# Last pair of a fused graph kernel: the attention result of group 0 finished by ScalarE and GpSimd instead of VectorE, with a new order of the last side work

## The chip, the cores and the metric

One core of a Trainium2 chip runs the whole kernel. The metric is the device time of one launch in microseconds (us). The profile shows one execution, with TensorE (PE), its weight loads (PEld), VectorE (DVE), ScalarE (ACT), GpSimd (POOL) and SyncE's DMA queue (SP) on one clock.

## The reference

For each of 128 graphs of 128 nodes with 256 features (f32):

```python
h = relu(layernorm(x))
for i in range(3):                       # gated graph network
    m = h @ weight[i]; aggr = A.T @ m    # A = (adj != 0)
    h = gru_cell(aggr, h, w_ih, w_hh, b_ih, b_hh)
x = x + h
h = relu(layernorm(x))                   # graph attention
Wh = h @ W.T
e = leaky_relu((Wh @ a1)[:, :, None] + (Wh @ a2)[:, None, :], 0.2)
att = softmax(where(adj == 0, -inf, e)); att = where(adj == 0, 0, att)
x = x + att @ Wh
```

## The kernel before, in words

Four graphs make a group, two groups (0 and 1) a pair, and there are 16 pairs. A pair runs through six slots: slot s works on group s % 2 in layer s // 2. Each slot has eight steps, hn0, r0, in0, z0, hn1, r1, in1, z1: the products of one gate for one half of the features, into a PSUM bank of the gate's own. ScalarE applies tanh, VectorE combines (`gate`, `update`). The state is kept in f16 high and low parts, so each product is three f16 matmuls.

All else is side work that is put between the steps: the neighbour sums (`neighbours`: PE, then an eviction by ACT, then the low part by DVE), the turning of the state by DMA, and the attention of the pair before (offset -1): norm, dot products, scores, softmax, `gather`, `attend`. Nothing orders it but tables written out by hand, `SIDE` for most pairs and `LAST` for the last pair. An entry such as `(4, 7): [("attend", 1, 0, -1)]` says that the engine does that stage, for group 1, half 0, of the pair before, after step 7 of slot 4. Each engine runs its own table strictly in order, and semaphores join them. So an entry that is moved also moves what is queued behind it on its engine. Key (6, 0) stands behind the last gate.

The last pair's own attention has nothing behind it to hide under, and has stages of its own, with f32 products. For group a and half h (two graphs), in the order of their needs:

- `residual` (PE L1088 turns the state, DVE L1382 adds it to x), `stats_att` (DVE L451), `tail_norm` (DVE L1494 to L1505, with a power on POOL, L1579), `tail_apply` (ACT L1276, the normed and clipped features);
- `tail_turn` (PE L1148), `tail_ut` (ACT L1290, out of PSUM), `tail_wh` (PE L1157, the product with W; the weights are put together once by POOL, L1582), `tail_out` (ACT L1296, out of PSUM);
- `tail_dots` (DVE L1511, two dot products per graph), `tail_row` (PE L1134, spreads one of them along a row), `tail_mask` (DVE L1520), `tail_scores` (DVE L1532 to L1545), `tail_softmax` (ACT L1284), `tail_scale` (DVE L1550 to L1554, one over the row sums, for a whole group);
- `tail_probs` (PE L1166, turns the probabilities), `tail_pt` (ACT L1302 or DVE L1481, out of PSUM), `tail_attend` (PE L1175), `tail_finish` (DVE L1461: product times row scale plus x, one instruction per graph), `tail_store` (SP L982).

Each half has its own PSUM banks. In the table before, DVE evicts `tail_pt` for half 1 of group 1 alone, and ACT the other three; all four `tail_finish` are DVE's.

Of the kernel before, what the change touches and what calls it, by code (L numbers as in the profile page):

```python
# [39 lines left out]
D = 256  # L40
# [176 lines left out]
        (4, 2): [("attend", 0, 1, -1), ("neighbours", 1, 2, 0, 0)],  # L217
        (4, 5): [("neighbours", 1, 2, 1, 0), ("gather", 1, 0, -1)],
        (4, 6): [("residual", 0, 0, 0)],
        (4, 7): [("gather", 1, 1, -1), ("attend", 1, 0, -1)],  # L220
        (5, 0): [("residual", 0, 1, 0)],
        (5, 1): [("attend", 1, 1, -1)],
        (5, 5): [("tail_row", 0, 0, 0)],
        (5, 7): [("tail_turn", 0, 0, 0), ("residual", 1, 0, 0), ("residual", 1, 1, 0), ("tail_probs", 0, 0, 0),
                 ("tail_turn", 0, 1, 0), ("tail_wh", 0, 0, 0), ("tail_row", 0, 1, 0), ("tail_attend", 0, 0, 0),
                 ("tail_wh", 0, 1, 0), ("tail_turn", 1, 0, 0), ("tail_turn", 1, 1, 0), ("tail_row", 1, 0, 0),
                 ("tail_wh", 1, 0, 0), ("tail_row", 1, 1, 0), ("tail_probs", 0, 1, 0), ("tail_wh", 1, 1, 0)],
        (6, 0): [("tail_probs", 1, 0, 0), ("tail_attend", 0, 1, 0), ("tail_attend", 1, 0, 0),
# [56 lines left out]
        (4, 0): [("neighbours", 0, 2, 1, 0), ("attend", 0, 0, -1), ("scores", 1, -1), ("update", 1, 1, 1, 0),  # L285
                 ("split_state", 1, 2, 1, 0), ("split_probs", 1, -1)],
        (4, 3): [("neighbours", 1, 2, 0, 0), ("attend", 0, 1, -1), ("update", 0, 2, 0, 0),
                 ("neighbours", 1, 2, 1, 0)],
        (4, 4): [("gather", 1, 0, -1)],
        (4, 5): [("residual", 0, 0, 0)],  # L290
        (4, 6): [("tail_mask", 0, 0), ("update", 0, 2, 1, 0), ("gather", 1, 1, -1), ("attend", 1, 0, -1),
                 ("residual", 0, 1, 0)],
        (4, 7): [("stats_att", 0, 0), ("tail_norm", 0, 0), ("attend", 1, 1, -1)],
        (5, 3): [("tail_dots", 0, 0, 0), ("tail_dots", 0, 1, 0), ("update", 1, 2, 0, 0)],
        (5, 4): [("tail_mask", 1, 0)],
        (5, 6): [("tail_scores", 0, 0, 0), ("update", 1, 2, 1, 0), ("residual", 1, 0, 0), ("residual", 1, 1, 0),
                 ("stats_att", 1, 0)],
# [40 lines left out]
def per_chunk(p, a, c):  # L338
    return p * 4 + 2 * a + c + 1
# [1274 lines left out]
```

## Time and profile before

| | |
|---|---|
| time, median of 3 runs (lowest to highest) | 1752.26 us (1751.38 to 1753.65) |
| time of the profiled execution, its span | 1753.62 us, 1751.8 us |
| PE busy | 1737.6 us, 99% of the span |
| DVE busy | 1489.7 us, 85% |
| ACT busy | 1106.5 us, 63% |
| POOL busy | 312.3 us, 18% |
| last gate product starts, last instruction on DVE starts | 1729.06 us, 1748.31 us |

An engine's row gives what it was busy in all. A kernel that keeps PE at 99% can only differ, under this change, in its last slots and behind the last gate; so the timelines of each engine are to be read there, item by item: start, duration, what it writes and reads, and in brackets how long the engine stood idle before and what released it. Durations of neighbouring items overlap a little, so the step from one start to the next is the cost of an item on a busy engine.

### The profile page before, as it was taken

The page shows a single profiled execution, that of the slowest core. Times are in us where ns is not written, and L with a number is a line of the kernel's source. Part 1 is how long each engine was busy: PE and PEld are TensorE (multiplying, and loading weights), DVE is VectorE, ACT ScalarE, POOL GpSimd, SP SyncE. Part 2 cuts the span into 40 slices and gives each one's busy share as a digit, 9 for nine tenths or more (in the row PEclk, how much of TensorE's full clock was granted, in tenths as well). Part 3 has the DMA queues.
Part 4 walks back from the last instruction along what each step waited for, and adds up shares of the span by engine and source line. Part 5 has one row for each costly group of instructions (what it writes and reads, how often), then busy time and mean ns, then how long its engine had stood idle before and what let it go on. Part 6 is the DMA issues. An engine that isn't in the chain of part 4 may idle for free. (4 is left out here: it accounts for less than half of the span.)

```text
span 1751.8 us, 32025 instructions
## 1 busy us (share of the span) xinstructions
PE 1737.6 (99%) x10109; PEld 907.3 (52%) x10109; DVE 1489.7 (85%) x2914; ACT 1106.5 (63%) x2009; POOL 312.3 (18%) x759
## 2 busy tenths in 40 slices
PE   8999999999999999999999999999999999999998
PEld 6444555545555454554545555455554545545455
DVE  6678898888988888888888988889888888888888
ACT  6566656666566666666666666665666666666664
POOL 2022022211212112021120222112121120211200
PEclk9999999999999999999999999999999999999999
DMA  4235352344425334253343523445243342533332
GB/s 121 67 61 103 80 125 43 90 106 88 111 42 116 82 84 111 42 123 84 72 114 75 123 48 82 109 90 114 42 112 86 84 108 42 122 85 74 79 67 67
DMA packets 393648, 152.03 MB, mean 87 GB/s; under 512 B 305280, under 2 KB 389776, under 8 KB 393616
## 3 DMA queue, kind: packets, MB, share of 16 engines
q1 hardware_dynamic: 393616, 151.64, 38.9%
q8 instruction: 16, 0.26, 0.1%
q14 instruction: 16, 0.13, 0.0%
HBM read 60.83 MB, written 16.84 MB: 44 GB/s over the span
## 5 line engine op out<-in xcount | busy, mean ns | idle before, releaser
L1203 ACT ACTIVATE n_out<-n_pre,smalls 128x512 f32<-128x512 f32 x192 | 137.8, 718 | 191.3 <-DVE n_pre L1330 190.6
L552 ACT ACTIVATE nb_hi<-nb_bank 128x512 f16<-128x512 f32 x192 | 114.1, 594 | 215.0 <-PE nb_bank L538 215.0
L523 PE MATMUL hn_bank<-ht_s,wh_hi 128*128 128x512 f16 x768 | 228.4, 379 | 0.0
L523 PE MATMUL r_bank<-ht_s,wh_hi 128*128 128x512 f16 x768 | 228.4, 379 | 0.0
L523 PE MATMUL z_bank<-ht_s,wh_hi 128*128 128x512 f16 x768 | 228.4, 379 | 0.0
L1198 ACT ACTIVATE tanh_r<-r_bank,b_rz,down 128x512 f32<-128x512 f32 x192 | 148.6, 774 | 112.4 <-PE r_bank L523 112.4
L1323 DVE SCALAR_TENSOR_TENSOR n_pre<-tanh_r,hn_b 128x512 f32<-128x512 f32 x192 | 147.3, 767 | 78.5 <-ACT tanh_r L1198 76.4
L556 DVE TENSOR_TENSOR nb_lo<-nb_bank,nb_hi 128x512 f16<-128x512 f32 x192 | 131.4, 684 | 47.5 <-ACT nb_hi L552 47.5
L1574 POOL TENSOR_TENSOR ht<-ht_s 128x512 f32<-128x512 f16 x64 | 85.9, 1342 | 467.3 <-DMA ht_s<-h_s 353.0
L1193 ACT ACTIVATE hn_b<-hn_bank,b_hn,down 128x512 f32<-128x512 f32 x192 | 147.9, 770 | 19.0 <-PE hn_bank L523 18.9
L1207 ACT ACTIVATE tanh_z<-z_bank,b_rz,down 128x512 f32<-128x512 f32 x192 | 147.6, 769 | 19.2 <-PE z_bank L523 19.0
L1330 DVE SCALAR_TENSOR_TENSOR n_pre<-in_bank,down,n_pre 128x512 f32<-128x512 f32 x192 | 143.1, 745 | 17.3 <-PE in_bank L523 14.8
L1343 DVE SCALAR_TENSOR_TENSOR diff<-tanh_z,diff 128x512 f32<-128x512 f32 x192 | 143.6, 748 | 10.6 <-ACT tanh_z L1207 3.5
L523 PE MATMUL hn_bank<-ht_s,wh_lo 128*128 128x512 f16 x384 | 145.5, 379 | 0.0
L523 PE MATMUL r_bank<-ht_s,wh_lo 128*128 128x512 f16 x384 | 145.5, 379 | 0.0
L523 PE MATMUL r_bank<-nb_hi,wi_hi 128*128 128x512 f16 x384 | 145.5, 379 | 0.0
L523 PE MATMUL r_bank<-nb_lo,wi_hi 128*128 128x512 f16 x384 | 145.5, 379 | 0.0
L523 PE MATMUL r_bank<-nb_hi,wi_lo 128*128 128x512 f16 x384 | 145.5, 379 | 0.0
L523 PE MATMUL in_bank<-nb_hi,wi_hi 128*128 128x512 f16 x384 | 145.5, 379 | 0.0
L523 PE MATMUL in_bank<-nb_lo,wi_hi 128*128 128x512 f16 x384 | 145.5, 379 | 0.0
L523 PE MATMUL in_bank<-nb_hi,wi_lo 128*128 128x512 f16 x384 | 145.5, 379 | 0.0
L523 PE MATMUL z_bank<-ht_s,wh_lo 128*128 128x512 f16 x384 | 145.5, 379 | 0.0
(350 smaller groups left out, 3794.9 us busy)
## 6 DMA issues: line engine op xcount, KB each, us to landing
x_in<-in_x_dram SPq DMA_DIRECT2D x32, 512.0 KB, 4.8
x_res<-in_x_dram SPq DMA_DIRECT2D x32, 512.0 KB, 4.4
out_dram<-x_out SPq DMA_DIRECT2D x30, 512.0 KB, 5.2
adj_in<-in_adj_dram SPq DMA_DIRECT2D x32, 256.0 KB, 5.6
adj_att<-in_adj_dram SPq DMA_DIRECT2D x32, 256.0 KB, 4.5
s_row<-s_dram SPq DMA_DIRECT2D x30, 256.0 KB, 3.5
h_s<-ht_s SPq DMA_TRANSPOSE x128, 3.1
ht_s<-h_s SPq DMA_TRANSPOSE x64, 3.3
```

The source lines that it names most:

```text
L523: last = nc.tensor.matmul(bank_ap, w, d, start=start and i == 0, stop=stop and i == len(todo) - 1)
L552: nc.scalar.activation(nb_hi[a][:, c, :], nb_bank[:], ACT.Copy).then_inc(nb_hi_ready, 1)
L556: nc.vector.tensor_tensor(nb_lo[a][:, c, :], nb_bank[:], nb_hi[a][:, c, :], ALU.subtract).then_inc(nb_lo_ready, 1)
L1193: nc.scalar.activation(hn_b[c][:], hn_bank[:], ACT.Identity, bias=b_hn[:, c:c + 1], scale=down_gate).then_inc(hn_ready, 1)
L1198: nc.scalar.activation(tanh_r[c][:], r_bank[:], ACT.Tanh, bias=b_rz[:, c:c + 1], scale=down_half).then_inc(tanh_r_ready, 1)
L1203: nc.scalar.activation(n_out[c][:], n_pre[c][:], ACT.Tanh, bias=bih[:, 4 + c:5 + c]).then_inc(n_ready, 1)
L1207: nc.scalar.activation(tanh_z[c][:], z_bank[:], ACT.Tanh, bias=b_rz[:, 2 + c:3 + c], scale=down_half).then_inc(tanh_z_ready, 1)
L1323: nc.vector.scalar_tensor_tensor(n_pre[c][:], tanh_r[c][:], 1.0, hn_b[c][:], ALU.add, ALU.mult).then_inc(rn_ready, 1)
L1330: nc.vector.scalar_tensor_tensor(n_pre[c][:], in_bank[:], down_gate, n_pre[c][:], ALU.mult, ALU.add).then_inc(n_pre_ready, 1)
L1343: nc.vector.scalar_tensor_tensor(diff[c][:], tanh_z[c][:], 1.0, diff[c][:], ALU.add, ALU.mult).then_inc(zdiff_ready, 1)
L1574: nc.gpsimd.tensor_tensor(ht[a][:, c, :], ht_s[0][a][:, c, 0, :], ht_s[0][a][:, c, 1, :], ALU.add).then_inc(ht_ready, 1)
```

## The change

`tail_finish` of group 0 goes from one fused VectorE instruction per graph to two steps: ScalarE writes product times row scale to `x_out`, and GpSimd adds x for two graphs at once. `tail_store` of group 0 waits for that. In the same diff the tables of the last pair get another order from slot 4 on: on PE, `tail_turn` (0, 0) and `tail_row` (0, 1) move ahead of the last two gate products, and the neighbour sums of group 1 and `residual` (0, 1) change places with other work; `tail_pt` of group 0 half 0 and of group 1 half 0 go from ACT to DVE; DVE does the scores of group 0 half 1 before the last state update; SP issues the stores of the pair before ahead of the loads for group 1. Unchanged lines are left out of the diff.

```diff
-        (4, 2): [("attend", 0, 1, -1), ("neighbours", 1, 2, 0, 0)],
-        (4, 5): [("neighbours", 1, 2, 1, 0), ("gather", 1, 0, -1)],
+        (4, 2): [("neighbours", 1, 2, 0, 0), ("attend", 0, 1, -1)],
+        (4, 5): [("gather", 1, 0, -1)],
...
-        (4, 7): [("gather", 1, 1, -1), ("attend", 1, 0, -1)],
-        (5, 0): [("residual", 0, 1, 0)],
+        (4, 7): [("gather", 1, 1, -1), ("neighbours", 1, 2, 1, 0), ("attend", 1, 0, -1), ("residual", 0, 1, 0)],
...
-        (5, 5): [("tail_row", 0, 0, 0)],
-        (5, 7): [("tail_turn", 0, 0, 0), ("residual", 1, 0, 0), ("residual", 1, 1, 0), ("tail_probs", 0, 0, 0),
-                 ("tail_turn", 0, 1, 0), ("tail_wh", 0, 0, 0), ("tail_row", 0, 1, 0), ("tail_attend", 0, 0, 0),
-                 ("tail_wh", 0, 1, 0), ("tail_turn", 1, 0, 0), ("tail_turn", 1, 1, 0), ("tail_row", 1, 0, 0),
-                 ("tail_wh", 1, 0, 0), ("tail_row", 1, 1, 0), ("tail_probs", 0, 1, 0), ("tail_wh", 1, 1, 0)],
-        (6, 0): [("tail_probs", 1, 0, 0), ("tail_attend", 0, 1, 0), ("tail_attend", 1, 0, 0),
+        (5, 3): [("tail_row", 0, 0, 0)],
+        (5, 5): [("tail_turn", 0, 0, 0), ("tail_row", 0, 1, 0)],
+        (5, 7): [("residual", 1, 0, 0), ("tail_turn", 0, 1, 0), ("tail_wh", 0, 0, 0), ("residual", 1, 1, 0),
+                 ("tail_wh", 0, 1, 0)],
+        (6, 0): [("tail_probs", 0, 0, 0), ("tail_probs", 0, 1, 0), ("tail_attend", 0, 0, 0), ("tail_turn", 1, 0, 0),
+                 ("tail_attend", 0, 1, 0), ("tail_row", 1, 0, 0), ("tail_turn", 1, 1, 0), ("tail_wh", 1, 0, 0),
+                 ("tail_row", 1, 1, 0), ("tail_wh", 1, 1, 0), ("tail_probs", 1, 0, 0), ("tail_attend", 1, 0, 0),
...
     "act": {
...
-        (4, 0): [("softmax", 1, -1), ("split_state", 1, 2, 1, 0)],
-        (4, 1): [("split_probs", 1, -1)],
-        (4, 2): [("neighbours", 1, 2, 0, 0)],
-        (4, 6): [("neighbours", 1, 2, 1, 0), ("gather", 1, 0, -1)],
-        (4, 7): [("gather", 1, 1, -1)],
-        (5, 2): [("tail_apply", 0, 0)],
-        (5, 7): [("tail_softmax", 0, 0, 0), ("tail_ut", 0, 0, 0), ("tail_out", 0, 0, 0), ("tail_pt", 0, 0, 0),
-                 ("tail_ut", 0, 1, 0), ("tail_apply", 1, 0), ("tail_ut", 1, 0, 0), ("tail_softmax", 0, 1, 0)],
-        (6, 0): [("tail_ut", 1, 1, 0), ("tail_out", 0, 1, 0), ("tail_out", 1, 0, 0), ("tail_pt", 0, 1, 0),
-                 ("tail_softmax", 1, 0, 0), ("tail_pt", 1, 0, 0), ("tail_softmax", 1, 1, 0), ("tail_out", 1, 1, 0)],
+        (4, 1): [("split_state", 1, 2, 1, 0)],
+        (4, 2): [("softmax", 1, -1), ("split_probs", 1, -1)],
+        (4, 6): [("gather", 1, 0, -1), ("neighbours", 1, 2, 0, 0)],
+        (4, 7): [("gather", 1, 1, -1), ("neighbours", 1, 2, 1, 0)],
+        (5, 1): [("tail_apply", 0, 0)],
+        (5, 6): [("tail_ut", 0, 0, 0)],
+        (5, 7): [("tail_softmax", 0, 0, 0), ("tail_ut", 0, 1, 0), ("tail_softmax", 0, 1, 0), ("tail_out", 0, 0, 0),
+                 ("tail_out", 0, 1, 0)],
+        (6, 0): [("tail_pt", 0, 1, 0), ("tail_apply", 1, 0), ("tail_ut", 1, 0, 0), ("tail_ut", 1, 1, 0),
+                 ("tail_finish", 0, 0, 0), ("tail_out", 1, 0, 0), ("tail_softmax", 1, 0, 0),
+                 ("tail_finish", 0, 1, 0), ("tail_softmax", 1, 1, 0), ("tail_out", 1, 1, 0)],
...
     "dve": {
...
-        (4, 0): [("neighbours", 0, 2, 1, 0), ("attend", 0, 0, -1), ("scores", 1, -1), ("update", 1, 1, 1, 0),
-                 ("split_state", 1, 2, 1, 0), ("split_probs", 1, -1)],
-        (4, 3): [("neighbours", 1, 2, 0, 0), ("attend", 0, 1, -1), ("update", 0, 2, 0, 0),
-                 ("neighbours", 1, 2, 1, 0)],
-        (4, 4): [("gather", 1, 0, -1)],
-        (4, 5): [("residual", 0, 0, 0)],
-        (4, 6): [("tail_mask", 0, 0), ("update", 0, 2, 1, 0), ("gather", 1, 1, -1), ("attend", 1, 0, -1),
-                 ("residual", 0, 1, 0)],
-        (4, 7): [("stats_att", 0, 0), ("tail_norm", 0, 0), ("attend", 1, 1, -1)],
-        (5, 3): [("tail_dots", 0, 0, 0), ("tail_dots", 0, 1, 0), ("update", 1, 2, 0, 0)],
-        (5, 4): [("tail_mask", 1, 0)],
-        (5, 6): [("tail_scores", 0, 0, 0), ("update", 1, 2, 1, 0), ("residual", 1, 0, 0), ("residual", 1, 1, 0),
-                 ("stats_att", 1, 0)],
-        (5, 7): [("tail_norm", 1, 0), ("tail_scores", 0, 1, 0), ("tail_dots", 1, 0, 0)],
-        (6, 0): [("tail_dots", 1, 1, 0), ("tail_scores", 1, 0, 0), ("tail_scale", 0, 0), ("tail_scores", 1, 1, 0),
-                 ("tail_finish", 0, 0, 0), ("tail_finish", 0, 1, 0), ("tail_scale", 1, 0), ("tail_pt", 1, 1, 0),
+        (4, 0): [("neighbours", 0, 2, 1, 0), ("update", 1, 1, 1, 0), ("scores", 1, -1), ("attend", 0, 0, -1)],
+        (4, 1): [("split_state", 1, 2, 1, 0), ("split_probs", 1, -1)],
+        (4, 3): [("attend", 0, 1, -1), ("update", 0, 2, 0, 0)],
+        (4, 5): [("gather", 1, 0, -1)],
+        (4, 6): [("neighbours", 1, 2, 0, 0), ("tail_mask", 0, 0), ("residual", 0, 0, 0), ("update", 0, 2, 1, 0),
+                 ("neighbours", 1, 2, 1, 0), ("residual", 0, 1, 0), ("gather", 1, 1, -1)],
+        (4, 7): [("stats_att", 0, 0), ("attend", 1, 0, -1), ("tail_norm", 0, 0), ("attend", 1, 1, -1)],
+        (5, 1): [("tail_dots", 0, 0, 0)],
+        (5, 2): [("tail_dots", 0, 1, 0)],
+        (5, 3): [("update", 1, 2, 0, 0), ("tail_scores", 0, 0, 0)],
+        (5, 6): [("tail_scores", 0, 1, 0), ("update", 1, 2, 1, 0), ("residual", 1, 0, 0), ("residual", 1, 1, 0),
+                 ("stats_att", 1, 0), ("tail_norm", 1, 0), ("tail_scale", 0, 0)],
+        (5, 7): [("tail_pt", 0, 0, 0), ("tail_mask", 1, 0), ("tail_dots", 1, 0, 0), ("tail_dots", 1, 1, 0),
+                 ("tail_scores", 1, 0, 0)],
+        (6, 0): [("tail_scores", 1, 1, 0), ("tail_pt", 1, 0, 0), ("tail_scale", 1, 0), ("tail_pt", 1, 1, 0),
...
     "pool": {
...
-        (4, 6): [("tail_norm", 0, 0)],
-        (5, 1): [("tail_weights", 0)],
-        (5, 7): [("tail_norm", 1, 0)],
+        (4, 0): [("tail_weights", 0)],
+        (4, 1): [("tail_norm", 0, 0)],
+        (4, 2): [("tail_norm", 1, 0)],
+        (4, 3): [("tail_finish", 0, 0, 0)],
+        (5, 6): [("tail_finish", 0, 1, 0)],
...
     "sp": {
...
-        (4, 0): [("transpose", 1, 2, 1, 0)],
-        (4, 2): [("probs_transpose", 1, -1), ("load_att", 0, 0)],
-        (4, 4): [("load_att", 1, 0)],
-        (4, 5): [("store", 0, -1), ("store", 1, -1), ("tail_store", 0, 0, 0), ("tail_store", 0, 1, 0),
-                 ("tail_store", 1, 0, 0)],
-        (5, 1): [("tail_store", 1, 1, 0)],
+        (4, 0): [("probs_transpose", 1, -1)],
+        (4, 1): [("transpose", 1, 2, 1, 0)],
+        (4, 2): [("load_att", 0, 0)],
+        (4, 4): [("store", 0, -1), ("store", 1, -1), ("load_att", 1, 0), ("tail_store", 0, 0, 0),
+                 ("tail_store", 0, 1, 0), ("tail_store", 1, 0, 0)],
+        (4, 7): [("tail_store", 1, 1, 0)],
...
+        tail_scaled, tail_added = sem("tail_scaled"), sem("tail_added")
...
         def for_halves(name):
...
                 def tail_store(p, a, half):
-                    sp.wait_ge(out_ready, per_chunk(p, a, half))
+                    if a == 0:
+                        sp.wait_ge(tail_added, half + 1)
+                    else:
+                        sp.wait_ge(out_ready, per_chunk(p, 0, half))
...
-                all_pairs(act, gate, {
+                def tail_finish(p, a, half):
+                    act.wait_ge(tail_attend_done[a][half], 1)
+                    act.wait_ge(row_scale_ready, per_group(p, a))
+                    act.wait_ge(out_stored[a], per_load(p - 1))
+                    for i in range(2):
+                        b = 2 * half + i
+                        last = nc.scalar.activation(x_out[a][:, b, :], tail_half_banks[a][half][:, i * D:(i + 1) * D],
+                                                    ACT.Copy, scale=row_scale[a][:, b:b + 1])
+                    last.then_inc(tail_scaled, 1)
+
+                all_pairs(act, gate, {"tail_finish": tail_finish,
+                    
...
+                def tail_finish(p, a, half):
+                    pool.wait_ge(tail_scaled, half + 1)
+                    graphs = half_graphs(half)
+                    nc.gpsimd.tensor_tensor(x_out[a][:, graphs, :], x_out[a][:, graphs, :], x_res[a][:, graphs, :],
+                                            ALU.add).then_inc(tail_added, 1)
+
                 def tail_weights(p):
...
-                    "tail_norm": tail_norm, "tail_weights": tail_weights}, SIDE["pool"], LAST["pool"])
+                    "tail_norm": tail_norm, "tail_weights": tail_weights, "tail_finish": tail_finish}, SIDE["pool"], LAST["pool"])
...
```

## Rows read from the trace of the kernel before

**Rows 1.** The page: the span

```profile
span 1751.8 us, 32025 instructions
```

**Rows 2.** PE timeline behind the last gate: start us, us, item, count, [idle before <-releaser]

```profile
1729.28 0.60 PE L1148 MATMUL w_bank<-ident,relu_att 128*128 128x128 f32 x4
...
1731.83 0.65 PE L1088 MATMUL in_bank<-ident,ht 128*128 128x128 f32 x4 [1.52 <-DVE ht L1346]
...
1742.23 1.89 PE L1157 MATMUL in_bank<-wa_full,u_t 128*128 128x256 f32 x8
...
1743.96 0.38 PE L1166 MATMUL z_bank<-ident,tail_prob 128*128 128x128 f32 x2
...
1744.18 1.03 PE L1175 MATMUL r_bank<-x_in,tail_pt 128*128 128x256 f32 x4
1745.04 1.03 PE L1175 MATMUL t_bank<-x_in,tail_pt 128*128 128x256 f32 x4
...
1747.17 1.10 PE L1175 MATMUL in_bank<-x_in,tail_pt 128*128 128x256 f32 x4 [0.88 <-DVE tail_pt L1481]
```

**Rows 3.** DVE timeline: the mask of group 1, then behind the last gate

```profile
1725.89 0.42 DVE L1520 TENSOR_SCALAR tail_prob<-adj_att 128x512 f32<-128x512 int32 x1
...
1730.36 0.69 DVE L1343 SCALAR_TENSOR_TENSOR diff<-tanh_z,diff 128x512 f32<-128x512 f32 x1 [0.50 <-ACT tanh_z L1207]
...
1732.60 0.69 DVE L1382 TENSOR_TENSOR x_res<-x_res,in_bank 128x512 f32<-128x512 f32 x1 [0.22 <-PE in_bank L1088]
...
1736.73 0.42 DVE L1532 TENSOR_TENSOR score<-hn_bank,s 128x256 f32<-128x256 f32 x1
...
1738.28 0.42 DVE L1511 CUSTOM_DVE_ANT_0 dot_terms<-relu_gnn,c 128x256 f32<-128x256 f32 x1
...
1741.04 0.42 DVE L1532 TENSOR_TENSOR hn_b<-z_bank,s 128x256 f32<-128x256 f32 x1
...
1742.58 0.22 DVE L1550 TENSOR_SCALAR tail_live<-tail_max,down 128x4 f32<-128x4 f32 x1
...
1743.02 0.42 DVE L1532 TENSOR_TENSOR hn_b<-nb_bank,s 128x256 f32<-128x256 f32 x1
...
1744.61 0.88 DVE L1461 SCALAR_TENSOR_TENSOR x_out<-w_bank,row_scale,x_res 128x256 f32<-128x256 f32 x2
...
1746.60 0.42 DVE L1481 COPY tail_pt<-nb_bank 128x256 f32<-128x256 f32 x1
...
1748.31 0.88 DVE L1461 SCALAR_TENSOR_TENSOR x_out<-in_bank,row_scale,x_res 128x256 f32<-128x256 f32 x2 [0.50 <-PE in_bank L1175]
```

**Rows 4.** PE at the seam of slots 4 and 5

```profile
1709.79 0.28 PE L523 MATMUL w_bank<-pt_s,u_hi 128*128 128x128 f16 x2
...
1713.07 0.60 PE L1088 MATMUL t_bank<-ident,ht 128*128 128x128 f32 x4
```

**Rows 5.** DVE timeline, same seam, the state update of group 0, half 1

```profile
1711.23 0.69 DVE L1343 SCALAR_TENSOR_TENSOR diff<-tanh_z,diff 128x512 f32<-128x512 f32 x1 [0.75 <-ACT tanh_z L1207]
```

**Rows 6.** ACT timeline behind the last gate

```profile
1736.80 2.08 ACT L1276 ACTIVATE relu_gnn<-x_res,ln_att 128x256 f32<-128x256 f32 x4 [0.53 <-DVE ln_att L1505]
...
1742.49 0.38 ACT L1302 ACTIVATE tail_pt<-hn_bank 128x256 f32<-128x256 f32 x1
```

**Rows 7.** POOL timeline, one such addition

```profile
1653.95 1.16 POOL L1574 TENSOR_TENSOR ht<-ht_s 128x512 f32<-128x512 f16 x1
```

**Rows 8.** SP timeline: loads for group 1, stores of the pair before

```profile
1719.80 0.37 SPq L990 DMA_DIRECT2D x_res<-in_x_dram  x1
```

**Rows 9.** DVE timeline at the moment of rows 7

```profile
1654.39 1.26 DVE L1323 SCALAR_TENSOR_TENSOR n_pre<-tanh_r,hn_b 128x512 f32<-128x512 f32 x1 [2.68 <-ACT tanh_r L1198]
```

**Rows 10.** Stretches: us, PE PEld DVE ACT POOL busy (x), PEclk, DMA share, GB/s

```profile
1735.00:1737.00 2.00, 1.17 (x6) 1.00 (x6) 0.84 (x6) 1.47 (x4) 1.02 (x1) 1.00 0.00 0
...
1749.00:1750.00 1.00, 0.00 (x0) 0.00 (x0) 0.18 (x1) 0.00 (x0) 0.00 (x0) 1.00 0.52 174
1750.00:1751.00 1.00, 0.00 (x0) 0.00 (x0) 0.00 (x0) 0.00 (x0) 0.00 (x0) 0.72 0.78 262
```

## The prediction

> **What bounds the kernel now.** I read the page first for the span [rows 1], then the timelines of PE, DVE, ACT and POOL over the last 60 us, item by item, and last the clock by stretches. PE works without a gap from the setup to the end of the last gate product, at 1729.28 [rows 2]; the first idle time it shows after that is the 1.52 us before 1731.83. So what the change moves about inside slots 4 and 5 costs nothing while PE stays fed, and what it moves ahead of the last gate product costs its PE time. Behind that product 22.5 us remain. They are a chain: last state update, `residual` (1, 1), norm of group 1, its features, dot products, scores, softmax, `tail_attend`, last `tail_finish` at 1748.31, store [rows 3]. From 1736.73 to 1747.8 DVE is busy throughout, and is what sets the pace there; PE waits for it only at the end (0.88 us before 1747.17). That is where work taken off DVE can pay, at most.
>
> I follow one chain of times in both kernels; a difference in the start of the last `tail_finish` is the difference in the span.
>
> **Part 1, the seam of slots 4 and 5.** PE's side work there keeps its sum, only its order changes. The one wait that I find new is for `residual` (0, 1). Before, it stood behind hn0 of slot 5, at 1713.07 [rows 4], long after the state was ready. Now PE comes to it before hn0. By its own sum PE finishes z1 of slot 4 at 1709.34 (before 1709.79; the 0.45 of `neighbours` (1, 2, 1) now stand behind it), then `gather` 0.67, `neighbours` 0.45, `attend` 1.31: it is there at 1711.77. The state needs z1, then a tanh, then two operations of 0.72. Before, the first of these began 1.44 after the end of z1 (1711.23 against 1709.79) [rows 4, 5], and behind the last gate of all 1.08 after it (1730.36 against 1729.28) [rows 2, 3]. That puts the state at 1711.86 to 1712.22, a wait of 0.1 to 0.45. I take 0.3.
>
> **Part 2, work put ahead of the last gate.** `tail_turn` (0, 0), four f32 transposes, and `tail_row` (0, 1), two. Two take 0.22 (1743.96 to 1744.18) [rows 2], four so 0.43. With Part 1 the last gate product ends at 1729.28 + 0.43 + 0.22 + 0.3 = 1730.23, 0.95 later. DVE's dots and scores for group 0 are on time for it by my sum (dots (0, 0) done at 1721.2, row (0, 0) due at 1721.6), with only 0.4 to spare.
>
> **Part 3, from the last gate to the features of group 1.** Before, `residual` (1, 1) began 2.55 after the gate's end. Now PE puts `residual` (1, 0) 0.43, `tail_turn` (0, 1) 0.43 and `tail_wh` (0, 0) 1.73 (1742.23 to 1743.96) in front of it, 2.59 in all: the state's wait is filled, and 0.04 is lost. DVE's scores (0, 1), moved ahead of the state update, end by 1730.05 and have 0.5 us to spare before the tanh of z. So DVE's addition is at 1730.23 + 3.36 = 1733.59 instead of 1732.60. From there to `tail_apply` the same 4.20 as before (1732.60 to 1736.80) [rows 3, 6]: 1737.79, and DVE is free again at 1737.72.
>
> **Part 4, DVE to the scores.** Before, DVE did scores (0, 1) there (1736.73 to 1738.28, 1.55) ahead of the dots. Now it does `tail_scale` (0), 0.44 (1742.58 to 1743.02), `tail_pt` (0, 0), 0.34 (1746.60, free again at 1746.94), and `tail_mask` (1), 0.42 long, 0.35 in step [rows 3]: 1738.85. The features of half 0 come at about 1738.9, two of four activations of 2.08 in all. So the dots begin at 1738.9 and, with 2.76 as before, end at 1741.66, only 0.6 later than before: of the 1.0 behind, 0.4 is won back.
>
> **Part 5, PE comes in as the late one.** `tail_attend` (0, 0) now waits for `tail_pt` (0, 0), which DVE can only make after `tail_scale` (0), at 1738.16. From DVE's copy to the product 0.57 passed before (1746.60 to 1747.17). So it starts at 1738.73. Behind it PE has, in this order, `tail_turn` (1, 0), `tail_attend` (0, 1), `tail_row` (1, 0), `tail_turn` (1, 1), `tail_wh` (1, 0), before `tail_row` (1, 1): 0.86 + 0.43 + 0.86 + 0.22 + 0.43 + 1.73 = 4.53 (0.86 is 1744.18 to 1745.04), so the row starts at 1743.26. From transposes on PE to DVE's use took 0.77 for four (1731.83 to 1732.60), so 0.55 for two: scores (1, 1) begin at 1743.81, where they began at 1743.02. DVE stood ready at 1743.20; it waits 0.6 for PE.
>
> **Part 6, the fused operation removed.** Scores (1, 1) end at 1745.40 (1.59 as before, 1744.61). DVE is then free of the two `tail_finish` of group 0, 1744.61 to 1746.19 before, 1.58. This is the gain meant. But it does not come through: PE has `tail_wh` (1, 1) until 1745.21, `tail_probs` (1, 0), then DVE copies at 1745.76, `tail_attend` (1, 0) 1746.33 to 1747.19, `tail_probs` (1, 1), DVE copies at 1747.74 (0.55), last product at 1748.31 (0.57), last `tail_finish` 1.14 behind it, at 1749.45. Softmax (1, 1) is ready by about 1746.5 and waits for PE. So 1749.45 against 1748.31: **1.1 us later**. Sum: +0.95 (gate) +0.04, -0.4 (DVE before the dots), +0.2 (PE's row), and +0.35 from there on, where 1.58 of relief meets a longer path through PE and an eviction more on DVE.
>
> **Part 7, what ACT, POOL and SP get.** ACT's two evictions of 128x256 per half are bounded by the copy of that size, 0.38 [rows 6]; 0.6 per half with overlap. They stand at about 1742.3 and 1744.7, ahead of softmax (1, 1) at 1745.5; nothing, unless they come later. If each waited its full 0.8, softmax would be 0.2 late, within its slack of 0.7. GpSimd's addition has as many elements as its addition of two f16 halves, 1.16 [rows 7]; f32 inputs can make it longer, bounded by double. I take 1.2: done at 1744.2 and 1746.7, both stores out before the last one needs SP at 1750.3. `tail_weights` moves to an idle time of POOL. On SP the loads for group 1 go behind two stores: issued at 1719.80 before [rows 8], the same or 0.5 later now, needed at 1732.65; moved bytes are the same. The loads for group 0 go behind both turning DMAs, some 0.4 later, with about 1 us to spare.
>
> **Two mechanisms to weigh.** First, the shared way into memory. In this trace an operation of DVE with two inputs in SBUF took 1.26 instead of 0.69 while POOL's addition ran, and ended 0.54 after that did [rows 7, 9]: it was held until POOL was through. Leaky and maximum of the scores are such operations. The Trainium skill, "SBUF — State Buffer", section "Who interferes with whom", has it that GpSimd and a VectorE instruction with two SBUF inputs exclude each other for the whole instruction, whichever started first; the trace agrees. By my times the first addition starts at 1742.95, when scores (1, 0) are in their last operation and DVE would then idle for PE until 1743.8; leaky starts at 1744.3. It just fits; half a microsecond off, it costs. Second, PE's clock. It is at full speed in every stretch up to the end, with waits of 1.5 and 0.9 us in it [rows 2, 10]. After the last product, which ends at 1748.3, it falls between 1750 and 1751, to 1.2 GHz. The changed kernel has PE idle from 1735.5 (`residual` (1, 1) at 1732.82 and its 0.50, `tail_wh` 1.73, two `tail_probs` 0.44) to 1738.73, 3.2 us, longer than either. The Trainium skill, "TensorE: Matmul & The Clock Gate", section "What's actually happening", says that an idle PE is throttled to half rate by default and that activity releases it; it speaks against this schedule.
>
> **The rivals.** (a) *Clock falls in that wait, and is given back.* PE's 4.53 of Part 5 run at half speed for two or three microseconds: +1.5, in all +2.6. For it: the fall 2 us after the last product. Against: the waits of 1.5 that kept it. 0.24. (b) *It falls and stays down to the end*: 4.53 doubled, and some 2.3 of PE's share of Part 6: +6.8, in all +7.9. This is the slower side; it decides from the point where the fall comes and PE is not found busy enough afterwards. 0.05. (c) *GpSimd's addition holds DVE* in the last maximum of scores (1, 0), which then end at 1744.3: +0.5, in all +1.6. 0.12. (d) *PE is not late*: latencies from PE to DVE are shorter than I took and the seam costs nothing, so DVE alone sets the pace. Then scores (1, 1) follow at once and end at 1744.8, softmax at 1745.8, copy 1746.3, last `tail_finish` at 1748.0: -0.3. 0.13. (e) A transfer or row of slots 4 and 5 comes late, PE stalls there for some us: slower, 0.02. Something of over 3.5 us that I don't see on the good side: 0.02. (f) The forecast: 0.42.
>
> **How the numbers follow.** The profiled execution took 1753.62, 1.36 above the median of 1752.26, its span 1751.8. The sum is made in it: 1754.7 for such an execution, and 1752.26 + 1.1 = 1753.4 for the median. 0.2%, about what a measurement of this kernel can tell from no change, is 3.5 us: (a), (c), (d) and the forecast all lie inside, 0.91; faster 0.02, slower 0.07. Low: (d) 1752.0 less 0.9 by which runs lie below the median, 1751.1. High: (a) 1754.9 and 1.4 by which they lie above: 1756.2.
>
> **What would show it.** Last gate product ending near 1730.2; a wait of PE of 0.1 to 0.45 before `residual` (0, 1); no wait before `residual` (1, 1); a wait of some 3 us before `tail_attend` (0, 0), with PEclk 1.00 behind it; DVE idle for 0.6 before scores (1, 1); last `tail_finish` 1.1 later. It is wrong if the f32 products double in length behind 1738, if a leaky or a maximum takes over 0.8, or if DVE has no idle time between dots and scores.

## The result, and the profile after

The changed kernel takes 1754.22 us in the median of 18 runs (1752.53 to 1755.84), the kernel before 1751.62 in 18 runs (1750.55 to 1753.65). The ratio is 1.0015, with a 95% interval of 1.0009 to 1.0022: 2.6 us slower, between 1.6 and 3.9. The 2.6 is inside the 3.5 us (0.2%) that the prediction named as too small to tell from no change. The forecast was 1.1 us; 2.6 is the number of rival (a), the fall of PE's clock.

The page of the profiled execution (1754.74 us), its first lines:

```profile
span 1752.9 us, 32027 instructions
...
PE 1737.9 (99%) x10109; PEld 908.0 (52%) x10109; DVE 1487.6 (85%) x2912; ACT 1106.8 (63%) x2011; POOL 315.2 (18%) x761
```

The span is 1.1 us longer than in [rows 1], but that is not the whole difference: this execution came to the last slots 1.4 us earlier than the profiled one before (PE ends `attend` (1, 0) at 1710.40 here and did so at 1711.77 there). Profiled executions differ by that much far ahead of the change (the changed kernel alone came to this point at 1710.40 in one and at 1709.17 in another, x11 below), so I compare stretches and not clock times. Three stretches make up the end of the kernel:

| stretch | before | after |
|---|---|---|
| end of `attend` (1, 0) to end of the last gate product | 17.51 | 18.35 |
| from there to the last `tail_finish` (the "tail" below) | 19.03 | 20.67 |
| from there to the end of the span ("behind") | 3.49 | 3.48 |
| sum of the differences | | +2.47 |

That agrees with the 2.6 of the medians. PE's timeline behind the last gate product (at 1728.75), to be held against [rows 2]:

```profile
1728.75 0.60 PE L1094 MATMUL t_bank<-ident,ht 128*128 128x128 f32 x4
1729.18 0.60 PE L1154 MATMUL r_bank<-ident,relu_att 128*128 128x128 f32 x4
1729.62 1.89 PE L1163 MATMUL w_bank<-wa_full,u_t 128*128 128x256 f32 x8
1731.35 0.61 PE L1094 MATMUL in_bank<-ident,ht 128*128 128x128 f32 x4
...
1733.74 0.38 PE L1172 MATMUL hn_bank<-ident,prob 128*128 128x128 f32 x2
1737.12 1.35 PE L1181 MATMUL w_bank<-x_in,tail_pt 128*128 128x256 f32 x4 [3.00 <-DVE tail_pt L1498]
1738.27 1.06 PE L1154 MATMUL t_bank<-ident,relu_gnn 128*128 128x128 f32 x4
1739.12 1.91 PE L1181 MATMUL r_bank<-x_in,tail_pt 128*128 128x256 f32 x4
1740.83 0.59 PE L1140 MATMUL z_bank<-ident,s 128*128 128x128 f32 x2
1741.25 0.60 PE L1154 MATMUL in_bank<-ident,relu_gnn 128*128 128x128 f32 x4
...
1743.42 0.38 PE L1140 MATMUL nb_bank<-ident,s 128*128 128x128 f32 x2
...
1746.36 1.10 PE L1181 MATMUL t_bank<-x_in,tail_pt 128*128 128x256 f32 x4 [0.61 <-DVE tail_pt L1498]
...
1748.29 1.10 PE L1181 MATMUL in_bank<-x_in,tail_pt 128*128 128x256 f32 x4 [0.61 <-DVE tail_pt L1498]
```

The wait for the state before `residual` (1, 1) (1.52 in [rows 2]) is gone, filled by `tail_wh` (0, 0). A wait of 3.00 stands before `tail_attend` (0, 0), and behind it `tail_attend` (0, 1) takes 1.91 where it took 1.03, `tail_turn` (1, 0) 1.06 where such take 0.60. From 1741.25 on the durations are the old ones. The stretches say why (columns as in [rows 10]: us, PE PEld DVE ACT POOL busy, PEclk, DMA share, GB/s):

```profile
1735.00:1737.00 2.00, 0.00 (x0) 0.00 (x0) 0.91 (x6) 0.74 (x2) 0.96 (x1) 1.00 0.00 0
1737.00:1739.00 2.00, 1.88 (x8) 1.63 (x9) 1.93 (x10) 1.33 (x3) 0.00 (x0) 0.71 0.03 8
1739.00:1741.00 2.00, 2.00 (x7) 1.51 (x6) 1.23 (x8) 0.60 (x1) 0.00 (x0) 0.50 0.00 0
1741.00:1743.00 2.00, 2.00 (x14) 1.85 (x13) 1.44 (x7) 1.11 (x3) 0.00 (x0) 0.94 0.00 0
1743.00:1745.00 2.00, 2.00 (x12) 1.74 (x11) 1.18 (x4) 1.60 (x7) 1.27 (x1) 1.00 0.01 4
```

PE did nothing at all from 1735 to 1737; the granted clock then is 0.71, 0.50 (1.2 GHz) and 0.94 of full speed, and 1.00 again from 1743. DVE's timeline, the rows that answer to [rows 3]:

```profile
1732.06 0.69 DVE L1399 TENSOR_TENSOR x_res<-x_res,in_bank 128x512 f32<-128x512 f32 x1 [0.22 <-PE in_bank L1094]
...
1737.38 0.42 DVE L1528 CUSTOM_DVE_ANT_0 dot_terms<-relu_gnn,c 128x256 f32<-128x256 f32 x1
...
1741.45 0.42 DVE L1549 TENSOR_TENSOR hn_b<-z_bank,s 128x256 f32<-128x256 f32 x1 [1.22 <-PE z_bank L1140]
...
1742.92 0.17 DVE L1562 TENSOR_SCALAR tail_neg<-tail_max 128x2 f32<-128x2 f32 x1
1743.84 0.42 DVE L1549 TENSOR_TENSOR hn_b<-nb_bank,s 128x256 f32<-128x256 f32 x1 [0.75 <-PE nb_bank L1140]
1744.30 0.54 DVE L1553 SCALAR_TENSOR_TENSOR hn_b<-hn_b 128x256 f32<-128x256 f32 x1
...
1746.54 0.54 DVE L1567 TENSOR_SCALAR tail_live<-tail_max,down 128x4 f32<-128x4 f32 x1 [0.33 <-ACT tail_prob L1290]
...
1747.71 0.42 DVE L1498 COPY tail_pt<-nb_bank 128x256 f32<-128x256 f32 x1 [0.36 <-PE nb_bank L1172]
...
1749.42 0.88 DVE L1478 SCALAR_TENSOR_TENSOR x_out<-in_bank,row_scale,x_res 128x256 f32<-128x256 f32 x2 [0.50 <-PE in_bank L1181]
```

DVE stood idle 1.22 before scores (1, 0) and 0.75 before scores (1, 1), both for PE. Before, it had no idle time there. Leaky (1744.30) took 0.54 instead of 0.42 and `tail_live` 0.54 instead of 0.22, beside GpSimd's two additions:

```profile
1743.30 1.27 POOL L1601 TENSOR_TENSOR x_out<-x_out,x_res 128x512 f32<-128x512 f32 x1 [7.34 <-ACT x_out L1317]
1745.78 1.26 POOL L1601 TENSOR_TENSOR x_out<-x_out,x_res 128x512 f32<-128x512 f32 x1 [1.22 <-ACT x_out L1317]
```

### The profile page after: what moved, and what is told of

Its sections match the earlier page's. It is cut to its first block, busy times and chain, and to the rows that moved or that the text cites. A ratio compares the mean times of both kernels' runs of the same rounds, so it can differ in the third digit from the quotient of the medians.

```text
span 1752.9 us, 32027 instructions
## 1 busy us (share of the span) xinstructions
PE 1737.9 (99%) x10109; PEld 908.0 (52%) x10109; DVE 1487.6 (85%) x2912; ACT 1106.8 (63%) x2011; POOL 315.2 (18%) x761
## 4 chain that ended last, share of the span: by engine, by line
PE 99%; DMA 0%; DVE 0%; SPq 0%; issue 0%; POOL 0%; DVEq 0%
PE r_bank L525 29%; PE z_bank L525 28%; PE hn_bank L525 14%; PE in_bank L525 14%; PE s_bank L525 4%; PE w_bank L525 3%; PE nb_bank L539 2%; PE nb_bank L540 2%; DMA rows<-in_L_gnn_a_dram 0%; PE t_bank L1163 0%; PE w_bank L1163 0%; PE in_bank L1163 0%; PE t_bank L775 0%; PE r_bank L1181 0%; PE t_bank L1094 0%
```

## The experiments

"Tail" and "behind" are the two stretches of the table, from the profiled execution of each kernel; time is the median against that of the kernel before on the same chip. A ratio of one session has an interval of about 0.0009 to both sides, 1.6 us. So single ratios don't settle a difference of one microsecond; the traces, and the kernels run beside each other, do.

| kernel | time, ratio (interval) | tail | behind | PEclk in the tail |
|---|---|---|---|---|
| before | | 19.03 | 3.49 | 1.00 |
| changed | 1.0015 (1.0009 to 1.0022) | 20.67 | 3.48 | falls to 0.50 |
| x11, changed again | 1.0011 (1.0002 to 1.0020) | 19.00 | 3.48 | 1.00 |
| x1, wait filled | 1.0005 (0.9996 to 1.0014) | 19.00 | 3.57 | 1.00 |
| x3, order only | 1.0015 (1.0006 to 1.0025) | 20.45 | 3.48 | falls |
| x4, turn put back | 1.0003 (0.9994 to 1.0012) | 19.01 | 3.52 | 1.00 |
| x2, finish only | 1.0008 (0.9999 to 1.0017) | 19.60 | 4.52 | 1.00 |
| x10, finish later | 1.0006 (0.9997 to 1.0015) | 18.76 | 4.98 | 1.00 |
| x5, mixed | 1.0002 (0.9993 to 1.0011) | 17.91 | 4.52 | 1.00 |
| x6, additions early | 1.0005 (0.9995 to 1.0014) | 19.57 | 3.50 | 1.00 |
| x9, store order | 0.9998 (0.9989 to 1.0007) | 17.91 | 4.26 | 1.00 |
| x8, VectorE alone | 0.9994 (0.9985 to 1.0003) | 17.89 | 3.57 | 1.00 |

### Is it the clock? x1, x7, x11, x4

Theory A says that the time above the forecast is the fall of PE's clock in the wait; theory B says that it is queueing alone (PE's order, evictions, GpSimd).

**x1_fill.** PE is given work in its wait:

```diff
-        (6, 0): [..., ("tail_probs", 0, 1, 0), ("tail_attend", 0, 0, 0), ...
+        (6, 0): [..., ("tail_probs", 0, 1, 0), ("tail_fill", 0, 0, 0), ("tail_attend", 0, 0, 0), ...
+                def tail_fill(p, a, half):
+                    pe.wait_ge(tanh_z_ready, per_gate(p, 1, LAYERS - 1, 1))
+                    for i in range(12):
+                        nc.tensor.matmul(z_bank[:], wh_hi[:, 0, 0:P], ht_s[0][1][:, 0, 0, :], start=True, stop=True)
```

> The changed kernel with 12 extra f16 matmuls of 512 columns (2.6 us, result unused, into the idle bank of gate z) put between tail_probs (0, 1) and tail_attend (0, 0), where PE stood idle for 3.0 us. Theory A, the clock: with PE at work there, PEclk stays 1.00 from 1737 to 1743, the products of tail_attend (0, 1) take 1.0 instead of 1.9, the gate's end to the last tail_finish takes 19.2 to 19.5 instead of 20.67 us, and the kernel is +1.0 to +1.3 us against before instead of +2.6. Theory B, queueing alone (PE's order, evictions, GpSimd): nothing changes, 20.7 us from the gate's end and +2.6, or 0.2 more if the extra products run over.

Measured: tail 19.00, time 1752.62 against 1751.49, +1.1 us. PE's timeline, the same products:

```profile
1733.64 2.75 PE L1179 MATMUL z_bank<-ht_s,wh_hi 128*128 128x512 f16 x12
1736.80 1.10 PE L1186 MATMUL w_bank<-x_in,tail_pt 128*128 128x256 f32 x4 [0.40 <-DVE tail_pt L1503]
1737.74 0.60 PE L1154 MATMUL t_bank<-ident,relu_gnn 128*128 128x128 f32 x4
1738.18 1.03 PE L1186 MATMUL r_bank<-x_in,tail_pt 128*128 128x256 f32 x4
```

More work on PE made the tail 1.67 us shorter; 19.00 is 0.2 below the range expected. `tail_attend` (0, 1) takes 1.03 again. This is what theory A says; queueing alone can't gain from added products. **x7_fill_only_before** was the same kernel under another label (its name says otherwise), profiled in one more execution.

> The same kernel as x1_fill once more, for a second look at its clock: theory A says PEclk 1.00 up to the last product in this execution too, theory B has nothing to say on it.

It showed PE idle for 0.41 in place of 3.00, a clock of 1.00 and once more a tail of 19.00.

**x11_changed_again.** The changed kernel, not edited.

> The changed kernel itself once more, on the same chip as the three others, for a second look at its clock: theory A expects the fall to half within the wait before tail_attend (0, 0) again, tail_attend (0, 1) at 1.9 instead of 1.03, and +2.6 us (2 to 3.2) against before.

The time was +1.7 us (1753.43 against 1751.70), with the widest spread of all, 1751.44 to 1756.47. And the profiled execution missed the expectation: with the same wait, the clock did not fall.

```profile
1735.89 1.10 PE L1181 MATMUL w_bank<-x_in,tail_pt 128*128 128x256 f32 x4 [2.99 <-DVE tail_pt L1498]
1736.83 0.60 PE L1154 MATMUL t_bank<-ident,relu_gnn 128*128 128x128 f32 x4
1737.26 1.03 PE L1181 MATMUL r_bank<-x_in,tail_pt 128*128 128x256 f32 x4
```

```profile
1734.00:1736.00 2.00, 0.11 (x1) 0.14 (x2) 1.14 (x6) 0.97 (x2) 0.73 (x1) 1.00 0.00 0
1736.00:1738.00 2.00, 2.00 (x12) 1.77 (x13) 1.92 (x12) 1.64 (x4) 0.00 (x0) 1.00 0.03 8
1738.00:1740.00 2.00, 2.00 (x14) 1.79 (x13) 1.93 (x9) 1.08 (x4) 0.00 (x0) 1.00 0.00 0
1740.00:1742.00 2.00, 2.00 (x12) 1.74 (x11) 1.52 (x7) 1.60 (x7) 1.29 (x1) 1.00 0.01 4
```

Its tail is 19.00 (the last `tail_finish` started at 1746.52, the gate's end was 1727.52) against 20.67 for the very same program. So the fall is no certain result of the 3.0 us wait, and where it came it cost 1.67 us. That is the cleanest evidence for theory A, as the program is the same in both and the tails differ in nothing that comes before the fall (whether the chip was the same is not on record).

How often the clock falls is less certain. The mean clock of a whole run is 0.998 or 0.999 in 39 of the 40 runs of the kernels with this wait (18 of 18 of the first measurement, 11 of 11 of x3, 10 of 11 here), and 1.000 in all 34 runs of x1, x7, x4 and x8. But 0.999 alone proves no fall in the wait: 20 of the 87 runs of the kernel before that were made beside the experiments have it too, and so do 9 of 22 of x2 and x10; the clock falls behind the last product too [rows 10], which lowers the mean. A mean of 0.998, in 14 of the 40, stands in no run of any other kernel. That the fall comes in most executions of the changed kernel is likely from this and from the medians, and shown in two of the three profiled executions with this wait (the first one and x3's).

**x4_turn_back.** Real work in the wait instead of idle products:

```diff
-        (5, 5): [("tail_turn", 0, 0, 0), ("tail_row", 0, 1, 0)],
-        (5, 7): [("residual", 1, 0, 0), ("tail_turn", 0, 1, 0), ("tail_wh", 0, 0, 0), ("residual", 1, 1, 0),
-                 ("tail_wh", 0, 1, 0)],
+        (5, 5): [("tail_row", 0, 1, 0)],
+        (5, 7): [("residual", 1, 0, 0), ("tail_turn", 0, 0, 0), ("tail_turn", 0, 1, 0), ("residual", 1, 1, 0),
+                 ("tail_wh", 0, 0, 0), ("tail_wh", 0, 1, 0)],
```

(ScalarE's `tail_ut` (0, 0) moves behind the last tanh with it.)

> The changed kernel with tail_turn (0, 0) behind the last gate product again and tail_wh (0, 0) behind residual (1, 1), so that PE's own work fills 1.7 us of its idle time. Theory A: idle 1.4 us before tail_attend (0, 0), no fall of the clock; gate 0.43 earlier, 19.2 to 19.5 from the gate's end: +0.6 to +0.9 against before. Theory B (no part for the clock): 20.7 from the gate's end, only the 0.43 gained: +2.1.

Measured: waits of 1.08 and 1.27, clock 1.00, tail 19.01 (again 0.2 below the range expected), time +0.65 us (1752.14 against 1751.49). In the trace the stretch up to the gate is 17.90 instead of 18.35: that is the 0.43 of `tail_turn` (0, 0) no longer ahead of the gate. The median is 0.48 below that of x1, which ran beside it; that agrees, but alone it is too small a difference for the timing to settle.

### The move or the order? x3, x2, x10

**x3_order_only.** VectorE does the fused operation again; all tables otherwise as changed.

```diff
-    "act": (6, 0): [..., ("tail_finish", 0, 0, 0), ..., ("tail_finish", 0, 1, 0), ...
-    "pool": (4, 3): [("tail_finish", 0, 0, 0)], (5, 6): [("tail_finish", 0, 1, 0)]
+    "dve": (6, 0): [("tail_finish", 0, 0, 0), ("tail_scores", 1, 1, 0), ("tail_pt", 1, 0, 0), ("tail_finish", 0, 1, 0), ...
```

> The changed kernel with its new order, in which VectorE does tail_finish of group 0 again with the fused operation (half 0 in its idle time before scores (1, 1), half 1 behind tail_pt (1, 0)). If the new order is the cost, as I hold: the same as the changed kernel within 0.3 us, +2.6 against before, clock at half in the same stretch. If ScalarE and GpSimd are the cost: 1 us or more better than the changed kernel.

Measured: 1754.18, +2.7 us, the wait of 3.00, a tail of 20.45, 0.2 shorter than with the move. So the cost is the order's, and under it the move to ScalarE and GpSimd gains nothing: VectorE has room for the fused operations while it waits for PE. The 0.2 itself says little, as the clock fell a little differently (`tail_attend` (0, 0) took 2.04 here and 1.35 there, (0, 1) 1.16 and 1.91).

**x2_finish_only.** The other half: the order of before, only the move.

```diff
-    "dve": (6, 0): [..., ("tail_finish", 0, 0, 0), ("tail_finish", 0, 1, 0), ("tail_scale", 1, 0), ...
+    "dve": (6, 0): [..., ("tail_scale", 1, 0), ...
+    "act": (6, 0): [..., ("tail_softmax", 1, 0, 0), ("tail_finish", 0, 0, 0), ("tail_pt", 1, 0, 0), ("tail_softmax", 1, 1, 0),
+                    ("tail_out", 1, 1, 0), ("tail_finish", 0, 1, 0)]
+    "pool": ("tail_finish", 0, 0, 0) and ("tail_finish", 0, 1, 0) behind ("tail_norm", 1, 0)
```

> The kernel before, with its order, in which only tail_finish of group 0 goes to ScalarE and GpSimd (ScalarE evicts half 0 behind softmax (1, 0) and half 1 behind tail_out (1, 1)). If the fused operations set the end of DVE's chain, the last tail_finish comes 1.6 us earlier: gate's end to last tail_finish 17.5 instead of 19.03. My theory: PE's products and softmax (1, 1) come next at once, tail_pt (1, 1) can only start 0.2 earlier: 18.8 to 18.9, -0.1 to -0.3 us in time. If GpSimd's additions hold DVE: leaky, maximum or tail_scale longer by up to 1.2 and the time up to +1.

Measured: tail 19.60, behind 4.52, time +1.8 us (1753.25 against 1751.49). Neither the full gain nor my 0.2, but the third case of the expectation, on another operation than the ones that I had named. On DVE:

```profile
1741.88 0.42 DVE L1552 SCALAR_TENSOR_TENSOR hn_b<-hn_b 128x256 f32<-128x256 f32 x1
1742.36 0.29 DVE L1556 CUSTOM_DVE_ANT_0 hn_b<-hn_b,tail_prob 128x128 f32<-128x128 f32 x1
...
1742.90 1.22 DVE L1561 TENSOR_SCALAR tail_neg<-tail_max 128x2 f32<-128x2 f32 x1
1745.07 0.23 DVE L1566 TENSOR_SCALAR tail_live<-tail_max,down 128x4 f32<-128x4 f32 x1 [0.94 <-ACT tail_prob L1290]
```

On POOL:

```profile
1742.84 1.26 POOL L1600 TENSOR_TENSOR x_out<-x_out,x_res 128x512 f32<-128x512 f32 x1 [7.94 <-ACT x_out L1317]
1746.32 1.27 POOL L1600 TENSOR_TENSOR x_out<-x_out,x_res 128x512 f32<-128x512 f32 x1 [2.22 <-ACT x_out L1317]
```

`tail_neg`, two elements per partition, took 1.22 instead of 0.17: it started 0.06 after GpSimd's addition and ended with it. Softmax (1, 1) waited for it. I had counted only operations with two inputs in SBUF as exposed; this one has a single input. The Trainium skill, "SBUF — State Buffer", section "Who interferes with whom", counts `tensor_scalar` among those that can take the shared way with one input as well; the trace agrees, with 1.22 for 0.17. The 1.0 us behind the tail has another cause, the stores: SP issues its stores in order, and that of group 0 half 1 waits for GpSimd's second addition, which ended at 1747.59, later than the last `tail_finish` began. How much of the 1.0 that is, x9 shows.

**x10_finish_later.** ScalarE evicts half 0 one place later, behind softmax (1, 1).

> As the version with tail_finish alone moved, but ScalarE evicts half 0 behind softmax (1, 1), so that GpSimd's addition doesn't meet DVE's tail_neg, which it held there for 1.05 us (1.22 instead of 0.17). The lock theory: tail_neg 0.17 again, softmax (1, 1) 1.0 earlier, gate's end to last tail_finish 18.8 to 18.9 instead of 19.59; but the additions end later than the last tail_finish, both stores of group 0 are late and those of group 1 behind them: 5 us or more from there to the end, +1 us or more in time. If the long tail_neg had another cause: it stays at 1.2 and 19.6.

Measured: tail 18.76, behind 4.98, time +1.0 us (1752.72 against 1751.70), all within 0.04 of what was expected, and `tail_neg` is short again:

```profile
1741.88 0.17 DVE L1561 TENSOR_SCALAR tail_neg<-tail_max 128x2 f32<-128x2 f32 x1
```

The run shows what the fused operations were worth without the collision: 0.27 us (19.03 to 18.76) for 1.58 us taken off DVE. And it shows the choice that GpSimd leaves here: early, it meets DVE's operations; late, the stores.

### Is there a better order? x5, x6, x9, x8

**x5_mixed.** From x4: `tail_pt` of group 0 on ScalarE, so that PE does both `tail_attend` of group 0 in its wait; then

```diff
-        (6, 0): [("tail_probs", 0, 0, 0), ("tail_probs", 0, 1, 0), ("tail_attend", 0, 0, 0), ("tail_turn", 1, 0, 0),
-                 ("tail_attend", 0, 1, 0), ("tail_row", 1, 0, 0), ("tail_turn", 1, 1, 0), ("tail_wh", 1, 0, 0),
-                 ("tail_row", 1, 1, 0), ("tail_wh", 1, 1, 0), ("tail_probs", 1, 0, 0), ("tail_attend", 1, 0, 0),
-                 ("tail_probs", 1, 1, 0), ("tail_attend", 1, 1, 0)],
+        (6, 0): [("tail_attend", 0, 0, 0), ("tail_attend", 0, 1, 0), ("tail_turn", 1, 0, 0),
+                 ("tail_turn", 1, 1, 0), ("tail_row", 1, 0, 0), ("tail_wh", 1, 0, 0),
+                 ("tail_row", 1, 1, 0), ("tail_wh", 1, 1, 0), ("tail_probs", 1, 0, 0), ("tail_probs", 1, 1, 0),
+                 ("tail_attend", 1, 0, 0), ("tail_attend", 1, 1, 0)],
```

and `tail_finish` (0, 0) back on VectorE, half 1 on ScalarE and GpSimd behind `tail_out` (1, 1).

> A version that should beat both: as with tail_turn (0, 0) behind the gate, and tail_pt of group 0 on ScalarE, so that PE does both tail_attend of group 0 while it waits for the features of group 1; tail_turn (1, 1) before the row; tail_probs (1, 1) before tail_attend (1, 0); DVE does tail_finish (0, 0) while it waits for softmax (1, 1), ScalarE and GpSimd do half 1 behind tail_out (1, 1). By my sum 17.9 to 18.2 us from the gate's end to the last tail_finish (before 19.03), gate end 0.35 later: -0.5 to -0.9 us against before. If the clock falls in a shorter wait too, or DVE isn't what sets the pace: 19 or more, 0 to +1.

Measured: tail 17.91, as summed, but time +0.4 us (1752.26 against 1751.85), not -0.5 to -0.9: behind is 4.52. I had left the stores out of the sum.

**x6_adds_early.** The same, with both halves on ScalarE and GpSimd behind `tail_ut` (1, 0) and (1, 1).

> The same order, but both tail_finish of group 0 on ScalarE and GpSimd, and early: GpSimd's two additions (1.27 each) fall beside DVE's dot products and scores of group 1, nearly all with two inputs in SBUF. If GpSimd and DVE exclude each other: single dot products, leaky or maximum operations of DVE last up to 1.3 longer, 1.2 to 2.5 us in all, and the last tail_finish comes 0.8 to 2 us later than in the mixed version. If they run side by side: the same time as the mixed version within 0.2, and no operation of DVE is longer than 0.5.

Measured: tail 19.57, 1.66 longer than x5, in the range expected if the two engines exclude each other; time +0.9. DVE's dot products:

```profile
1738.66 0.08 DVE L1527 DVE_READ_ACCUMULATOR2_ANT s<- 128x1 f32 x1
...
1739.01 1.48 DVE L1527 CUSTOM_DVE_ANT_0 dot_terms<-relu_gnn,c 128x256 f32<-128x256 f32 x1
...
1740.87 1.02 DVE L1552 SCALAR_TENSOR_TENSOR hn_b<-hn_b 128x256 f32<-128x256 f32 x1
```

and GpSimd's two additions:

```profile
1738.81 2.80 POOL L1600 TENSOR_TENSOR x_out<-x_out,x_res 128x512 f32<-128x512 f32 x2 [3.77 <-ACT x_out L1316]
```

The last dot product took 1.48 and leaky 1.02, where their neighbours take 0.42: they were held by the first and the second addition. Two additions of 1.3 us on GpSimd cost VectorE 1.66 us; the four fused operations that they replace cost it 1.58.

**x9_store_order.** x5 with the store of (1, 0) issued ahead of that of (0, 1).

> The mixed version with the store of group 1 half 0 issued ahead of that of group 0 half 1, which waits for GpSimd. If SP stood behind GpSimd's addition: 4.52 falls to 3.5 to 4.0 behind the last tail_finish, and the time by 0.5 to 1 us against the mixed version (+0.4), so -0.1 to -0.6 against before. If it is the transfers themselves: no change, +0.4.

Behind fell to 4.26 only, where 3.5 to 4.0 was expected, and the time to -0.55 us (1751.15 against 1751.70). The traces split the 1.0 us in two. From the end of the last `tail_finish` to the end of the last issue on SP it takes 0.40 before, 0.88 in x5 and 0.60 here; the store of (0, 1) is still issued last but one. From there to the end of the span it takes 2.21 before, 2.76 in x5 and 2.78 here, and the slowest of the four stores lands 2.7 us after its issue in x2, x5, x9 and x10, against 2.2 before, in the changed kernel and in x8. So the waiting behind GpSimd's addition is about half of it and the order takes back 0.28; the other half is slower transfers. In all four the stores are issued close together, and the DMA engines are 1.03 to 1.05 busy in one microsecond, where it is 0.98 at most before. That this crowding is what slows them is likely, not shown.

**x8_dve_only.** x5 with nothing on ScalarE and GpSimd:

```diff
+        (5, 7): [("tail_mask", 1, 0), ("tail_one", 0, 0), ("tail_dots", 1, 0, 0), ...
+        (6, 0): [("tail_scores", 1, 1, 0), ("tail_pt", 1, 0, 0), ("tail_one", 1, 0), ("tail_one", 2, 0), ("tail_scale", 1, 0),
+                 ("tail_pt", 1, 1, 0), ("tail_one", 3, 0), ("tail_finish", 1, 0, 0), ("tail_finish", 1, 1, 0)],
```

`tail_one` is the fused operation for one graph of group 0.

> The mixed version's order for PE and ScalarE, but tail_finish of group 0 wholly on VectorE with the fused operation, one graph at a time in DVE's idle times: graph 0 before the dot products of group 1, graphs 1 and 2 behind tail_pt (1, 0), graph 3 behind tail_pt (1, 1). Nothing on GpSimd, stores in time. If the gain of the mixed version was lost behind its last tail_finish (4.52 us to the end of the span there, 3.49 before): 17.9 to 18.1 from the gate's end, 3.5 behind it, gate 0.35 later: -0.6 to -0.9 us against before. If ScalarE and GpSimd are needed for the gain: 0 or slower.

Measured: tail 17.89, behind 3.57, time 1750.76 against 1751.70, -0.9 us, ratio 0.9994 (0.9985 to 1.0003). The interval takes in 1, so the timing alone doesn't show a gain; the trace has 1.14 less in the tail, gives 0.39 back ahead of the gate (17.90 against 17.51) and 0.08 behind, 0.67 less in all. Its span, 1748.3, is the shortest of all. It is the version that I would keep, and the change named in the title is not part of it.

## Why the prediction was right or wrong

The time lay in the range and within 0.2%, as forecast, but the mechanism of the forecast was not the one that came. The forecast had PEclk 1.00 through the wait (0.42, against 0.24 for a fall that is given back), on the ground that waits of 1.5 us had kept it, so in its sum the clock costs nothing; it cost 1.67 us. The sign that the prediction gave for being wrong was there, the f32 products behind 1738 took 1.91 for 1.03 and 1.06 for 0.60. Rival (a) happened, with the number given for it, +2.6. That the number fits so well is in part luck: it was 1.1 for the order and 1.5 for the clock, and the traces have 0.80 (0.84 ahead of the gate, -0.03 in the tail of x11, -0.01 behind) and 1.67. So the sum without the clock was 0.3 too high. The +1.1 us of x1, which has the clock held up, is the forecast number, but its interval is 1.6 to both sides, and its trace has 0.88.

- **Part 1**, the wait before `residual` (0, 1): 0.13 measured (PE free at 1710.40, start at 1710.53) against 0.3 taken, range 0.1 to 0.45. DVE's use of the tanh of z came 1.09 after PE had ended z1 (1709.06 against 1707.97), as behind the last gate of all (1.08), the nearer of the two rows.
- **Part 2**: the stretch to the last gate product is 0.84 longer; 0.95 was summed. The wait of Part 1 is 0.17 shorter than taken, and `residual` (0, 1) took 0.49 in step behind it instead of 0.43. No row or dot product of group 0 was late.
- **Part 3**: `residual` (1, 1) 2.60 after the gate (2.59 summed), DVE's addition 3.31 after it (3.36), `tail_apply` 4.20 behind that (4.20). Right.
- **Part 4**: dots at 8.63 after the gate (8.67). Right: 0.35 to 0.4 won back.
- **Part 5**: `tail_attend` (0, 0) 8.37 after the gate (8.50), a wait of 3.00. From there to `tail_row` (1, 1) 6.30 instead of 4.53. This is the term of the sum that failed: with the clock held, in x11, it was 4.62, so 1.68 of the 1.77 are the clock's. PE's row was at DVE's use after 0.42, not 0.55, and DVE's wait for it, 0.6 in the sum, was 0.38 in x11.
- **Part 6**: right in kind. The 1.58 taken off DVE are worth 0.27 in x10 and nothing under the new order (x3), as PE's products and one softmax stand right behind.
- **Part 7**: GpSimd's addition took 1.27 (1.2 taken, bounded by double), ScalarE's pair of evictions 0.83, 0.7 in step (0.6). Rival (c) did not come on the path: leaky lost 0.12, `tail_live` 0.32 that `tail_probs` (1, 1) hid. But it is real, x2 and x6 show it at 1.05 and 1.66 us. In the change itself the addition began 0.38 after `tail_neg` (1, 0) had begun, at 1742.92. That gap is the slow clock's doing: with the clock at full speed, in x11, x1, x7 and x4, the two begin within 0.01 of each other, and `tail_neg` took its 0.17 in all four. In x2 the addition was first by 0.06, and `tail_neg` took 1.22. So rival (c) was missed very narrowly. In x11:

```profile
1740.39 0.17 DVE L1562 TENSOR_SCALAR tail_neg<-tail_max 128x2 f32<-128x2 f32 x1
1740.39 1.29 POOL L1601 TENSOR_TENSOR x_out<-x_out,x_res 128x512 f32<-128x512 f32 x1 [5.66 <-ACT x_out L1317]
```

- The stores of group 0 were in time in the changed kernel (3.48 behind), as said.

Not tried: a wait between 1.5 and 3.0 us, and the seam's 0.13 taken out. Why the clock fell in one execution of the same program and not in another stays open.

## What to carry to other kernels

Work moved out of a wait and ahead of a saturated PE is paid twice: once as PE time, and again if the clock falls in the wait it leaves behind; look at what is left in the wait, and fill it. An operation taken off an engine is worth only the room up to the next thing that is late, here 0.27 of 1.58 us, so follow the chain to the next engine before moving it. GpSimd is no free place for an addition while VectorE works out of SBUF: place it where VectorE reads PSUM or idles, or don't move it (in x10 the additions ran beside a copy out of PSUM and fused operations with one input in PSUM, and these took their usual 0.42 and 0.87), and look at the stores that then wait for it.

## What the runs showed of the hardware that I had not expected

- The same program with the same 3.0 us wait of PE had its clock at half in one profiled execution and at full in the other; 20.67 and 19.00 us of tail. Waits of 1.0 to 1.5 us showed no fall in any of the profiled executions; the mean clocks of the timed runs don't settle whether it ever comes there (0.999 in 29 of 109 runs of the kernels with the wait of 1.52, before, x2 and x10).
- GpSimd's addition held a VectorE operation on two elements, with one input in SBUF, for 1.05 us (x2), when the addition had begun 0.06 earlier; where the small operation began with it or 0.01 ahead of it, it took its 0.17 (x11, x1, x7, x4).
- Stores that wait for a slow producer lengthened the end of the kernel by 1.0 us (4.52 against 3.49, x2 and x5): about half is SP issuing in order, half slower landing (2.7 us from issue against 2.2).
